# Mixtures of twelve matrices: dense products with a weight against rows sent to blocks by indirect DMA

## The reference

```
# layer 0
x = x + xattn0(layernorm(x), ctx)             # 16 heads, projections Wq Wk Wv Wo with biases
def ffn0(x):                                  # on layernorm(x); 8192 tokens
    xa = x @ P_w.T
    C1, C2, C3 = (route(xa, U) for U in (U1, U2, U3))   # softmax over the best 3 of 12, else 0
    h = gelu(sum(C1[:, e] * (x @ W1[e].T) for e in range(12)))
    return sum(C2[:, e] * (h @ W2[e].T) for e in range(12)) + C3 @ b2
x = x + ffn0(layernorm(x))
# layer 1
x = x + xattn1(layernorm(x), ctx)             # 16 heads, no projections
x = x + moe(layernorm(x))                     # 64 experts, best 8, capacity 128 rows each, and a shared expert
```

## Time and profile before

| what | value |
|---|---|
| median of the runs | 2823.03 us |
| span of the profiled execution | 2796.0 us (the page gives no other time of it) |
| PE busy | 2627.6 us, 94%, 22949 matmul records |
| DVE busy | 2229.3 us, 80% |
| ACT busy | 1074.1 us, 38% |
| POOL busy | 808.2 us, 29% |
| DMA queues of SP / of POOL | 42.4% / 3.9% of the 16 engines' span |
| moved by DMA | 336.02 MB, mean 120 GB/s |

### The profile page before, as it was taken

The page is one execution under the profiler, slowest core; times in us unless marked ns, Lnnn a source line. Parts: engine busy times, 40 slices in busy tenths (PEclk is TensorE's granted clock), DMA queues, the critical chain, the costliest instruction groups (busy, mean ns, idle before and its releaser), DMA issues.

```text
span 2796.0 us, 59981 instructions
## 1 busy us (share of the span) xinstructions
PE 2627.6 (94%) x22949; PEld 2189.7 (78%) x22949; DVE 2229.3 (80%) x6135; ACT 1074.1 (38%) x1622; POOL 808.2 (29%) x829
## 2 busy tenths in 40 slices
PE   3899999999999999999999999999999999985999
PEld 2788788888888888888888888888888888763776
DVE  5678788888888888888888888888888888762554
ACT  3333334444434444433444444444443444322232
POOL 1000132322223222222222222322222232226444
PEclk9999999999999999999999999999999999986999
DMA  7644444444444434443444444343444343245997
GB/s 224 175 136 105 113 123 130 123 110 111 117 116 108 116 107 100 116 110 94 110 103 97 114 116 109 105 116 101 96 108 98 92 107 71 58 87 155 231 234 168
DMA packets 322210, 336.02 MB, mean 120 GB/s; under 512 B 46676, under 2 KB 302751, under 8 KB 321412
## 3 DMA queue, kind: packets, MB, share of 16 engines
q1 hardware_dynamic: 286404, 307.37, 42.4%
q0 software_dynamic: 33792, 18.52, 3.9%
q10 hardware_dynamic: 1728, 6.29, 0.7%
HBM read 191.65 MB, written 221.81 MB: 148 GB/s over the span
## 4 chain that ended last, share of the span: by engine, by line
PE 76%; DVE 17%; issue 3%; DMA 2%; POOL 1%; ACT 1%; SPq 1%; POOLq 0%; ACTq 0%; DVEq 0%
PE mixp L1447 34%; PE attn_out L1381 6%; DVE nm L1039 6%; PE first L1347 5%; PE second L1365 4%; DVE hid L1131 4%; PE misc L1315 3%; PE mixp L1549 3%; PE misc L1273 3%; PE misc L1483 2%; PE second L1568 2%; PE misc L1522 2%; PE misc L1392 2%; DVE xhat L1000 2%; PE first L1504 2%
## 5 line engine op out<-in xcount | busy, mean ns | idle before, releaser
L739 POOL DMA_INDIRECT expert_slots<-row_mem,sidx x512 | 507.2, 991 | 1065.1 <-PE first L1347 769.5
L854 ACT ACTIVATE exps<-second 128x1024 f32<-128x1024 f32 x512 | 525.7, 1027 | 735.8 <-PE second L1365 727.7
L1447 PE MATMUL mixp<-w_h,r_part_h 128*128 128x256 f32 x3072 | 666.8, 298 | 10.9 <-DVE hid L1131 6.1
L1039 DVE TENSOR_REDUCE nm<-first 128x4 f32<-128x1024 f32 x504 | 613.7, 1218 | 27.0 <-PE first L1347 23.6
L1447 PE MATMUL mixp<-w_h,r_part_l 128*128 128x256 f32 x3072 | 610.9, 280 | 0.0
L1447 PE MATMUL mixp<-w_l,r_part_h 128*128 128x256 f32 x3072 | 610.3, 280 | 0.0
L1447 PEld LDWEIGHTS mixp<-w_h,r_part_h 128*128 128x128 f32 x3072 | 469.0, 189 | 60.5 <-DVE hid L1131 22.2
L1447 PEld LDWEIGHTS mixp<-w_l,r_part_h 128*128 128x128 f32 x3072 | 469.7, 188 | 0.0
L1447 PEld LDWEIGHTS mixp<-w_h,r_part_l 128*128 128x128 f32 x3072 | 469.6, 188 | 0.0
L1131 DVE SCALAR_TENSOR_TENSOR x_mem<-mixp,C,x_mem 128x256 f32<-128x256 f32 x768 | 334.7, 477 | 75.4 <-PE mixp L1447 72.0
L1131 DVE SCALAR_TENSOR_TENSOR hid<-mixp,C,hid 128x256 f32<-128x256 f32 x704 | 301.5, 476 | 97.0 <-PE mixp L1447 96.8
(11 more groups left out here) (236 smaller groups left out, 3585.9 us busy)
## 6 DMA issues: line engine op xcount, KB each, us to landing
kst<-k_parts SPq DMA_DIRECT2D x256, 192.0 KB, 4.0
qst<-q_parts SPq DMA_DIRECT2D x256, 192.0 KB, 4.5
q_parts<-nat_h SPq DMA_DIRECT2D x128, 256.0 KB
k_parts<-ctx_part_h SPq DMA_DIRECT2D x64, 256.0 KB, 2.5
k_parts<-nat_h SPq DMA_DIRECT2D x64, 256.0 KB, 5.6
q_parts<-nat_l SPq DMA_DIRECT2D x64, 256.0 KB
exps<-in_wgu SPq DMA_DIRECT2D x30, 384.0 KB, 4.0
expert_slots<-row_mem SPq DMA_DIRECT2D x16, 642.0 KB, 6.3
```

The source lines that it names most:

```text
L739: pool.e.indirect_dma_start(out=slots_dram, out_offset=bass.IndirectOffsetOnAxis(ap=sidx[b % 2][:, t, k:k + 1], axis=0), in_=row[b % 2][:, ...
L854: act.e.activation(exps[:, j % NU, :, :, :].rearrange("p k t s -> p (k t s)"), second[:, :, :].rearrange("p k s -> p (k s)"), ACT.Exp, sca ...
L1039: dve.e.tensor_reduce(nm[u % 2][:, :, 2 * j:2 * j + 2].rearrange("p t k -> p k t"), (mixp_mem if in_mixp(b, kind, j) else first)[:, :, :]. ...
L1447: m = pe.e.matmul(mixp[q % 2][:, t * D:(t + 1) * D], src[i][:, dt, t * P:(t + 1) * P], wmix[n][j][:, l, dt, :], start=(k == 0), stop=(k == ...
```

## The change

- A mixture no longer multiplies all tokens with all matrices. For a group of four batches (GROUP) each token's three chosen matrices are known; ranks are counted (`r_pos`: PE counts with matmuls, DVE makes positions), and POOL sends each token's row three times into a DRAM buffer sorted by matrix (`x_send`, 6 indirect DMAs a batch). A table (`table`, `place`) says where each 128-row block starts and which matrix it has. Unused rows are padded with zeros (`pads`).
- Per group and mixture there are 18 pairs of blocks (GROUP_PAIRS). For a pair SP loads 2 x 128 rows (`m_load`; for the first mixture at a row number that it reads from the table in DRAM into registers), PE turns them and ACT copies (`m_turn`), PE multiplies by the matrix whose address comes from a register (`m_mm`, plain fp32, four matmuls), ACT copies the result, SP stores it. POOL gathers each token's three results (`gather`), DVE weighs and adds them (`sum`). Between the two mixtures gelu's rows are sent again (`h_send`).
- Projections, routing and the mixtures use plain fp32 products; scores alone keep the three terms. The splits and most copies of weights go.
- x after layer 0 is stored to DRAM and loaded again, since layer 1 of a batch now runs beside layer 0 of the batch 15 later (LEAD).
- Each engine has its own order of pieces (ORDERS), not a common one. exps has 3 buffers for 4 (NU), mixture results one bank (mix_y) for two. Scatters no longer wait for the scores (t_s1). The max rows go in two DMAs for four. Kept experts are loaded straight from the inputs.

```diff
+LEAD = 15
+GROUP = 4
+GROUP_PAIRS = 18
+PASSES = ((0, 0), (0, 1), (1, 0), (2, 0), (1, 1), (2, 1), (3, 0), (3, 1), (4, 0), (4, 1), (5, 0), (5, 1), (6, 0), (6, 1), (7, 0), (7, 1))
...
+    sp_order, pool_order, act_order, dve_order, pe_order = (
+        list(pieces(NB, L, NE, e)) for e in ("sp", "pool", "act", "dve", "pe"))
...
+                elif what == "m_load":
+                    q, = a
+                    g, n, i = pair_at(q)
...
+                    sp.wait_ge(c_mout[q % NM], 16 * (q // NM))
+                    if n == 0:
+                        sp.e.reg_load(row_regs, table_dram[g, 1:2, 2 * i:2 * i + 2])
+                    for t in range(2):
+                        if n == 0:
+                            src = to_first[g % 2][bass.ds(sp.e.snap(row_regs[t], min_val=0, max_val=ALL_ROWS), P), :]
+                        else:
+                            src = to_second[g % 2][(2 * i + t) * P:(2 * i + t + 1) * P, :]
+                        sp.e.dma_start(m_rows[q % NM][:, t, :], src).then_inc(c_mrow[q % NM], 16)
+                elif what == "m_mm":
...
+                    sp.e.dma_start(dst[2 * i * P:2 * (i + 1) * P, :].rearrange("(t p) d -> p t d", p=P),
+                                   m_rows[q % NM]).then_inc(c_mout[q % NM], 16)
...
                 elif what == "max_rows":
                     kind, b, J, h, u = a
                     sp.wait_ge(a_mT, u + 1)
-                    for part in range(2):
-                        for k in range(2):
-                            r0 = (part * 2 + k) * HP
-                            sp.e.dma_start(row_block(q_st[u % 3], k, K1 + part, 1),
-                                           mT[u % 2][r0:r0 + HP, :].bitcast(F32)).then_inc(c_m[u % 2], 16)
+                    for k in range(2):
+                        sp.e.dma_start(row_block(q_st[u % NST], k, K1, 2), mT[u % 2][2 * HP * k:2 * HP * (k + 1), :].bitcast(
+                            F32)).then_inc(c_m[u % 2], 16)
...
+                elif what == "x_send":
...
+                    for t in range(TILES):
+                        for k in range(KR):
+                            pool.e.indirect_dma_start(
+                                out=to_first[g % 2], out_offset=bass.IndirectOffsetOnAxis(ap=slot_no[:, b % NROUTE, 0, t, k:k + 1], axis=0),
+                                in_=xhat[1][:, t, :], in_offset=None, bounds_check=ALL_ROWS - 1,
+                                oob_is_err=False).then_inc(c_send, 16)
+                elif what == "gather":
...
+                    for k in range(KR):
+                        pool.e.indirect_dma_start(
+                            out=g_rows[i][:, k, :], out_offset=None,
+                            in_=of_first[b // GROUP % 2] if n == 0 else of_second[b // GROUP],
+                            in_offset=bass.IndirectOffsetOnAxis(ap=slot_no[:, b % NROUTE, n, t, k:k + 1], axis=0),
+                            bounds_check=BLOCK_ROWS - 1, oob_is_err=False).then_inc(c_gather[i], 16)
...
-                        src = mixp[q % 2][:, t * D:(t + 1) * D]
-                        c = Cw[b % 2][:, t, n, l:l + 1]
...
+                elif what == "sum":
...
+                            if n == 0 and k == 0:
+                                dve.e.tensor_scalar(rows_[:, 0, :], rows_[:, 0, :], c, None, ALU.mult).then_inc(done, 1)
+                            else:
+                                acc = rows_[:, 0, :] if n == 0 else xc(b)[:, t, :]
+                                dve.e.scalar_tensor_tensor(acc, rows_[:, k, :], c, acc, ALU.mult, ALU.add).then_inc(done, 1)
...
-                    for t in range(TILES):
-                        k = 0
-                        for i, j in TERMS:
-                            for dt in range(DT):
-                                m = pe.e.matmul(mixp[q % 2][:, t * D:(t + 1) * D], src[i][:, dt, t * P:(t + 1) * P],
-                                                wmix[n][j][:, l, dt, :], start=(k == 0), stop=(k == 3 * DT - 1))
...
+                elif what == "m_mm":
...
+                    if i % 2 == 0:
+                        pe.e.reg_load(regs, table_dram[g, 2 * n:2 * n + 1, 2 * i:2 * i + 4])
+                    pe.wait_ge(a_mh, q + 1)
+                    pe.wait_ge(a_my, q)
+                    for t in range(2):
+                        part = pe.e.snap(regs[2 * (i % 2) + t], min_val=0, max_val=(L - 1) * DT * D)
+                        for dt in range(DT):
+                            m = pe.e.matmul(mix_y[:, t * D:(t + 1) * D], m_T[q % NMT][:, dt, t * P:(t + 1) * P],
+                                            wflat[n][:, bass.ds(part + dt * D, D)], start=(dt == 0), stop=(dt == DT - 1))
```

More of the change, by code:

```diff
@@ new lines, in job_order, with instances @@
+def job_order(NB):
+    jobs = [("A", b) for b in range(LEAD)]
+    for b in range(NB):
+        jobs.append(("C", b))
+        if LEAD + b < NB:
+            jobs.append(("A", LEAD + b))
+    return jobs
+def instances(NB):
+    NG = NB // GROUP
+    found = {k: [(k, b) for b in range(NB)] for k in A_KINDS + C_KINDS + ["gelu", "h_send", "place"]}
+    for k in "ARCD":
+        for n in ("ln1", "ln2"):
+            found[n + k] = [(n, k, b) for b in range(NB)]
+    for n in range(2):
+        found[f"gather{n}"] = [("gather", n, b, t) for b in range(NB) for t in range(2)]
+        found[f"sum{n}"] = [("sum", n, b) for b in range(NB)]
+    found["scatter"] = [("scatter", b, i) for b in range(NB) for i in range(16)]
+    for k in ("table", "pads"):
+        found[k] = [(k, g) for g in range(NG)]
+    for k in ("m_load", "m_turn", "m_mm"):
+        found[k] = [(k, q) for q in range(2 * NG * GROUP_PAIRS)]
+    for k in ("keep", "empty"):
+        found[k] = [(k, i) for i in range(16)]
+    for k, count in HALF_KINDS.items():
+        found[k] = [(k, kind, b, J, h, 2 * J + h) + ((i,) if count > 1 else ())
+                    for J, (kind, b) in enumerate(job_order(NB)) for h in range(2) for i in range(count)]
+    return found
@@ L238, in pieces @@
+def pieces(NB, L, NE, engine=None):
+    found = instances(NB)
+    if engine is None:
+        for k in found:
+            yield from found[k]
+    else:
+        rest = {k: iter(v) for k, v in found.items()}
+        for letter in ORDERS[engine]:
+            yield next(rest[LETTERS[letter]])
     for e in range(NE + 3):
@@ L482, in q_parts_of, with gathered, gather_count, gather_free @@
             return sum(2 if kind == "A" else 1 for (kind, _), j in job_J.items() if j <= J)
-        def in_mixp(b, kind, j):
-            return j % 2 == 1 and (kind, b) in (("A", 0), ("C", NB - 1))
+        def gathered(n, b, t):
+            r = 2 * b + t
+            return r % NG1 if n == 0 else NG1 + r % NG2
+        def gather_count(n, b, t):
+            return 16 * KR * ((2 * b + t) // (NG2 if n else NG1) + 1)
+        def gather_free(n, b):
+            return (c_hsend[b % 2], 16 * 2 * KR * (b // 2)) if n == 0 else (v_s2, 2 * KR * b)
+        passes = list(PASSES)
+        def pair_at(q):
+            return passes[q // GP] + (q % GP,)
+        def pass_end(g, n):
+            return (passes.index((g, n)) + 1) * GP
+        def stored_by(g, n):
+            return [(c_mout[i], 16 * len(range(i, pass_end(g, n), NM))) for i in range(NM)]
+        def placed_no(b):
+            return (2 + GROUP) * (b // GROUP) + 3 + b % GROUP
         def ring_no(e):
@@ L534, in store_parts @@
                         sem_, 16)
-            for c in range(FIRST):
-                sp.e.dma_start(stage[c][:, 0:chunks[c][2]], chunks[c][1]).then_inc(c_stage[c], 16)
+            pad_regs = [sp.e.alloc_register(f"pad_row{i}") for i in range(4)]
+            row_regs = [sp.e.alloc_register(f"block_row{t}") for t in range(2)]
+            for dst, src in ((wo, woT_in), (wkv, wkvT_in), (wq, wqT_in)):
+                sp.e.dma_start(dst[:, :, :], src).then_inc(c_w, 16)
             slots = slots_dram.rearrange("(e c) f -> c e f", c=CAP)
-            for what, *a in order:
+            for what, *a in sp_order:
@@ L701, in gpsimd_program @@
             pool.e.memset(minus_half[:, :], -0.5).then_inc(p_const, 1)
-            for what, *a in order:
+            for what, *a in pool_order:
                 if what == "ctx_split":
@@ L1500, in tensor_program @@
                     b, = a
-                    claim("first", (v_h2, b + 1))
+                    claim("first", (v_h, 2 * b + 2))
+                    pe.wait_ge(a_dt, b + 1)
                     for t in range(TILES):
```

1187 lines of the change are left out of this document (670 added, 517 removed), and 69 rows, old and new, of tables (HALF_PLACES, LAST, OPENING).

## The result

The changed kernel takes 3763.4 us (median of four runs, 3752.6 to 3768.6), the kernel before beside it 2824.2: a ratio of 1.333, interval 1.330 to 1.335. Forecast were 2540 us and a range up to 2760. The profiled execution has a span of 3750.5 us at a mean granted clock of 0.80 (before 0.98).

A forecast was written before the change was run, and what follows sets the result against it. Each stage was bounded by its largest engine, PE 448, PE 1156 (POOL and DMA within 3%) and POOL 507 us: 2111 / 0.92 = 2295. Expert loop 216 and 27 more make 2538, say 2540 us; range 2380 to 2760.

The forecast's parts named there:

- stage AC: Middle stage, 17 batches of each layer: PE 1156 us, POOL 1141, DMA 1129, so PE the largest.
- stands beside PE: In the stage with both layers, POOL at 1.28 us an indirect DMA comes to 1141 us, PE to 1156.
- The sum: Largest engine of each stage, 448 + 1156 + 507 = 2111 us, over 0.92 is 2295, plus 216 and 27: 2538.
- PE's prices: Matmul groups priced from one stretch's chain, such as 1.73 us for plain fp32; 1864 us over three stages.
- stage C: Last stage, layer 1 of 15 batches alone: POOL largest at 507 us, PE 353; the lower clock may come there.
- What would show it: Closing list of signs of being right or wrong; wrong includes gathers well over 1.28 us and low clock in AC.
- register loads: 144 new loads of four registers from DRAM on PE, priced at 0.64 us each; PE becomes 448, 1156, 353.
- the 0.92: Share of its bounds the new kernel was taken to reach, against 0.93 to 0.94 before: 2111 / 0.92 = 2295 us.
- Slower: Outcome of a kernel slower than before, chance 0.12 in all, 0.09 of it by max rows standing behind bulk work.
- max rows behind bulk work: Rival on SP's queue: each of 128 halves loses up to 4.0 us; with 3.0 it is 2922 us; chance 0.10.
- SP's wait for the copy: SP stood 978 us for ACT's copy before, 7.6 each time; after, this wait holds block loads behind it too.
- Indirect rows were dear: Rival: gathers cost POOL 1.85 us each (2744 us) or data 5.89 us/MB (2750 us); chance 0.20.

The follow-up runs named there:

- e3: Kernel before with the scatters' wait for the scores (t_s1) left out; 3061 us, ratio 1.084.
- e8: Kernel before without the scatters' wait, with one small power on POOL after each scatter, so they start 2.0 us apart; 2822 us, ratio 0.997.
- e6: Kernel after with its 1280 indirect DMAs ahead of the expert loop replaced by small memsets on POOL; 2985 us, ratio 1.053.
- e14: Kernel before without the scatters' wait, each scatter cut to 64 of its 128 rows; 3054 us, ratio 1.080.
- e1: Kernel after with the ring (scratch memory for POOL's DMAs) at 4096 instead of 2048; 3802 us, ratio 1.348 to before.
- e2: Kernel before with the ring (scratch memory for POOL's DMAs) at 2048 instead of 4096; 2812 us, ratio 0.996.

## Why the prediction was wrong

**The step that failed is that POOL, in stage AC, "stands beside PE".** The sum took the largest engine of each stage and let POOL's 1.28 us an indirect DMA run beside the rest for nothing. Each took 1.28 to 1.36 as priced, POOL's 1485 busy and about 1280 x 0.30 of issue are 1869 ahead of the loop for 1835, and the queue's new data went at (0.119 x 3750 - 0.039 x 2796) / 100.7 MB = 3.35 us/MB for 3.17. The duration was right; what an indirect DMA does to the other engines was not in the sum: without the 1280, the time is 778 us less, of the 1223 by which the forecast missed. PE's late updates, 18% of the chain of after, are the part that the traces show. The rest of the 778, the order on POOL and the queue's data, is not told apart from them.

In particular, the dropped `t_s1` wait was counted as neither cost nor gain. Its removal was plain in the change, and POOL's timeline of before shows what it did: scatters released one by one by PE. Alone it costs 238 us (e3), and a spacing in its place gives them back (e8). Against this reading stood: there 48 scatters go 1.28 us apart, and not one update of PE is late. So a row is not sufficient by itself. What else it takes stays open; in e3 two rows at the end of the batches, of 16 and 28, had late updates for 12 and 8 us.

**PE's prices and clock: 445 us** (2985 - 2540, and as much by busy time ahead of the loop, 2309 for 1864). The prices came from one stretch of a kernel whose PE hardly waits, where a group overlaps the end of the one before. The chain of e6 has the same pieces behind a wait and in a train:

```profile
1092.92 0.22 PE mixp L1533 x2
1093.14 1.79 PE mixp L1639 x8
1094.93 0.02 issue
1094.96 0.59 ACT mixrow L971
1095.55 0.13 issue
1095.69 1.99 PE mixp L1639 x8
1097.68 0.44 PE mixp L1570 x4
1098.11 0.43 PE second L1543 x4
```

The products of a pair are 1.99 behind a wait, for 1.73. Second scores are 0.43 in most places where they don't follow the first ones directly, for 0.24, and the kernel before had shown that: over its whole chain they are under 0.3 in 197 of 199 places behind first scores, and 0.4 to 0.5 in 158 of 164 behind other matmuls. In the chain of e6 only 54 stand behind first scores. In the 150 of 275 stretches of 10 us of e6 at the full clock PE makes 69.0 matmuls in 9.24 us busy, which is 2110 us for all 15752: 246 more than priced. The other 199 are put down to its stretches at the lower clock. This is an estimate, since the pieces are not mixed alike everywhere. Of the clock I had said that it may come in stage C; it came in all three, 0.87, 0.89 and 0.84 without indirect DMAs, 0.84, 0.80 and 0.73 with them, one of the signs of being wrong that "What would show it" names.

**Waits: near in size, in part by luck.** The sum allowed 2295 - 1864 = 431 us beside PE's work; e6 has 437. But of the 431, 154 were POOL's lead over PE in stage C (507 - 353), which e6, without indirect DMAs, doesn't have; 93 were register loads and 184 the 0.92. By construction 2540 + 445 + 778 = 3763.

**Register loads: right.** PE's 144 take 0.50 to 1.47 us, median 0.51, together 88 for 92. The floor of about 600 ns that the Trainium skill gives ("DMA: Bandwidth & Descriptors", section "Latency and other measured facts") is near, but 101 of the 144 lie below it, and the measurement decides.

**Rivals.** Slower came true by another way than the one described. The max rows behind bulk work were hardly a cause: in the kernel after PE's second scores wait 13.4 us for qst<-mT in all. SP's wait for the copy fell as expected, from 978 us to:

```profile
SPq L688 <- ACT mT L978: 402.9, 66, 35.5
```

Indirect rows were dear, but not in POOL's time nor in data, the two prices that rival had. The expert loop was right.

## What to carry to other kernels

Price an indirect DMA by what it does to the engines that wait for PE, not only by POOL's time. Keep POOL's from running in rows, by a wait on the engine that they disturb or by other POOL work between, and place them where nothing waits behind: spacing gave back all of 238 us where nothing did, and at most 89 where something did. A wait that seems idle may be what keeps two engines apart: before it goes, ask what it spaces. Prices read from a train of matmuls don't hold where each piece stands behind a wait or behind another kind of piece.

## What was not expected of the hardware

- Rows of indirect DMAs 1.28 us apart go with updates of PE that come up to some 20 us late, in the stretch shown one in 4 to 8 us; 2.0 us apart hardly any do (17 to 39 us in all), and it goes with the number, not with 64 or 128 rows each (e3, e14). The Trainium skill ("SBUF — State Buffer", section "SBUF: two separate sides") has PE waiting for no one on its ports. Here PE's updates stand still beside POOL's indirect DMAs, but whether a port of SBUF, PSUM or the semaphores is the place was not tried, so the runs neither bear that out nor refute it. Nor was it tried whether the recording plays a part, which misses updates in kernels where indirect DMAs follow each other on POOL without standing behind PE (some 250 of PE's 3009 in after, 210 of 3201 in e8, where hardly one is late).
- A larger ring made the kernel after 1% slower (e1); a smaller one made the kernel before 0.4% faster (e2).
